# A fused Perceiver layer on one core: stage 1 in another order, an fp32r gate, and a scratch tensor by channel quarters

## The reference, cut to what matters

```python
def _L0_xattn_ref(encoder_hc, decoder_hq, w_sim, b_sim, W_qv, b_qv):      # hc = layernorm(x), hq = context
    w1, w2, w3 = (w_sim[:d], w_sim[d:2 * d], w_sim[2 * d:])
    Sim = (hc @ w1)[:, :, None] + (hq @ w2)[:, None, :] + einsum('bid,bjd->bij', hc * w3, hq) + b_sim[0]
    hq_hat = einsum('bij,bjd->bid', softmax(Sim, axis=2), hq)
    hc_bar = einsum('bi,bid->bd', softmax(max(Sim, axis=2), axis=1), hc)[:, None, :]
    return concatenate([hc, hq_hat, hc * hq_hat, hc * hc_bar], axis=-1) @ W_qv + b_qv

def _L0_attn_ref(x, A, Bp, Cp, Dp, Wg, bg, gamma, beta):                  # x = layernorm(x)
    xg = x * sigmoid(x @ Wg.T + bg)
    # for each channel: s = s @ A + xt * Bp;  y = s . Cp + Dp * xt, over 32 tokens
    return layernorm(y + xg) * gamma + beta

def _L0_ffn_ref(x, fast_b, w_fc, w_proj, u, v, gate):                     # x = layernorm(x)
    h = bitlinear(x, w_fc) + gate * (x @ v.T @ fast_b.T @ u.T)            # ternary weights times a row scale
    return bitlinear(relu(h) ** 2, w_proj)
```

## Time and profile before

| what | value |
|---|---|
| median of three runs | 539.21 us (538.7 to 541.0) |
| profiled execution | 538.89 us, span 536.4 us, clock 0.98 |
| instructions | 13420 |
| busy: PE, DVE, ACT, POOL | 479.4, 419.9, 359.4, 343.9 us |
| stage 1, step 1's hq transposes to step 32's | 28.9 to 334.3 us |
| first scan block | 339.7 us |

### The profile page before, as it was taken

How to read it: one execution, slowest core, us unless ns; L and a number is a source line. 1 busy time by engine, 2 the same in 40 slices (tenths; PEclk the granted TensorE clock), 3 DMA queues, 4 the chain that set the end, 5 groups by cost and what they waited for, 6 DMA issues and landing times. The chain is left out here.

```text
span 536.4 us, 13420 instructions
## 1 busy us (share of the span) xinstructions
PE 479.4 (89%) x4310; PEld 402.2 (75%) x4310; DVE 419.9 (78%) x1159; ACT 359.4 (67%) x854; POOL 343.9 (64%) x444
## 2 busy tenths in 40 slices
PE   2397799999999999999999996876799999999996
PEld 2275687888887877687787875765588888888885
DVE  1398888888888999999998884457677987988654
ACT  2555578676876767677676766555578768768753
POOL 1377767676775757756756664503578878888653
PEclk9789999999999999999999999998899999999999
DMA  6734445756584555555645568259502022011102
GB/s 206 197 114 149 138 151 160 219 156 217 145 234 136 177 169 139 191 146 139 199 136 144 194 200 178 60 133 218 125 1 79 1 80 79 26 55 39 41 1 78
DMA packets 81316, 70.38 MB, mean 131 GB/s; under 512 B 39760, under 2 KB 64608, under 8 KB 81248
## 3 DMA queue, kind: packets, MB, share of 16 engines
q1 hardware_dynamic: 81248, 69.54, 45.4%
HBM read 56.87 MB, written 12.65 MB: 130 GB/s over the span
## 5 line engine op out<-in xcount | busy, mean ns | idle before, releaser
L1647 POOL TENSOR_TENSOR sq_lo<-scan_x,sq_hi 128x512 fp32r<-128x512 f32 x63 | 82.7, 1313 | 33.6 <-ACT sq_hi L1619 33.6
L705 PE MATMUL turn_ps<-ident,ctxn 128*128 128x128 f32 x512 | 70.3, 282 | 4.4 <-DMA ctxn<-in_ctx 4.4
L933 ACT COPY ctxT<-turn_ps 128x512 f32<-128x512 f32 x128 | 68.2, 583 | 5.4 <-PE turn_ps L705 5.4
L705 PEld LDWEIGHTS turn_ps<-ident,ctxn 128*128 128x128 f32 x512 | 58.2, 144 | 18.0 <-issue 13.2
L1611 ACT ACTIVATE relu<-fc_ps,fc_square 128x512 f32<-128x512 f32 x64 | 43.8, 684 | 31.0 <-PE fc_ps L1545 30.9
L1689 DVE SCALAR_TENSOR_TENSOR scan_x<-fc_ps,relu 128x512 f32<-128x512 f32 x64 | 43.8, 684 | 26.0 <-ACT relu L1611 25.5
L1121 POOL TENSOR_TENSOR hc_lo<-hc_probT,hc_hi 128x256 fp32r<-128x256 f32 x32 | 23.4, 731 | 61.0 <-ACT hc_hi L942 60.9
L1541 PE MATMUL fc_ps<-xn_hi,fc_T 128*128 128x512 f32 x128 | 52.1, 407 | 2.1 <-DVE scan_x L1689 2.1
L1107 POOL TENSOR_TENSOR rstd<-ve,neg_half 128x1 f32<-128x1 f32 x64 | 35.2, 550 | 27.6 <-DVE ve L1331 17.7
L1541 PE MATMUL fc_ps<-xn_lo,fc_T 128*128 128x512 f32 x128 | 51.1, 399 | 0.0
L1113 POOL TENSOR_TENSOR proj_in<-proj_in,below 128x512 f32<-128x512 f32 x31 | 49.3, 1592 | 0.0
(11 more groups left out here) (227 smaller groups left out, 1400.8 us busy)
## 6 DMA issues: line engine op xcount, KB each, us to landing
ctxn<-in_ctx SPq DMA_DIRECT2D x32, 1024.0 KB, 5.5
resid<-in_x SPq DMA_DIRECT2D x32, 128.0 KB, 5.2
ctx_end<-in_ctx SPq DMA_DIRECT2D x32, 128.0 KB
gated_tokens<-gated SPq DMA_DIRECT2D x32, 128.0 KB, 6.2
scan_x<-gated_tokens SPq DMA_DIRECT2D x60, 64.0 KB, 4.9
out<-resid SPq DMA_DIRECT2D x7, 512.0 KB, 3.1
scan_tokens<-scan_x SPq DMA_DIRECT2D x12, 256.0 KB, 5.1
y_in<-scan_tokens SPq DMA_DIRECT2D x4, 512.0 KB, 4.8
```

The source lines that it names most:

```text
L705: mm = pe.transpose(turn_ps[b % 2][:, (c * JT + t) * P:(c * JT + t + 1) * P], ctxn[p][:, b, t, c * P:(c + 1) * P], ident[:, :])
L933: act.copy(ctxT[:, b, :, 0:J - 1], turn_ps[b % 2][:, :].rearrange("p (k j) -> p k j", k=KD)).then_inc(ctxT_copied, 1)
L1647: pool.tensor_tensor(sq_lo[:, m, :], sq[m % SQ], sq_hi[:, m, :].bitcast(F32), ALU.subtract).then_inc(sq_lo_done, 1)
```

## The change

What it does, part by part:

1. TensorE's step has another order: context 0 and 1, prob's transposes, pool, projection of hc, context 2 and 3, attend, score, z's transposes, hq's transposes, projection of hb, hc's transposes of the next group, gate, projections of hq and hcq. A projection waits for its lo half only in front of the matmuls that read it.
2. The gate is 6 fp32r matmuls with zT_hi, zT_lo, wgT_hi, wgT_lo. VectorE makes zT_lo every step.
3. The context has three buffers; the third is lent from rows 0 to 15 of `toeplitz`, which is zeroed in eight parts, six in steps 4 to 9 and two in step 31.
4. The first loads come in another order, and wqv_hi waits for W_qv alone and is made in step 1 (as is wqv_lo, after hcqT).
5. The ternary halves of w_fc alternate over steps 17 to 32 and stand ahead of hq on VectorE; magnitudes and scale come two steps earlier.
6. The state product stands at the end of GpSimd's step; steps 3, 4 and 5 have a second one ahead of hb_lo; the product with C comes in step 29.
7. On ScalarE hc's copy of the next group and hcwT stand before and behind the softmax exponential, and hc_hi at the end.
8. VectorE's step has another order, given in the diff.
9. In the end of stage 1 the placing, turn_z and the gate of the last group stand elsewhere between the scan blocks.
10. The y scratch is ordered by quarters of the channels: stores have 8 KB contiguous for each partition, a y load is four DMAs with pieces of 256 B; y load 0 is issued ahead of the last `gated` store.

```diff
+        def y_load(sp, c):
+            piece, part = divmod(c, 2)
+            for r in range(CH):
+                src = bass.AP(tensor=scan_dram.tensor, offset=piece * PB * L * D + (part * TOK + r * P) * CQ,
+                              ap=[[CQ, P], [PB * L * CQ, NB], [1, CQ]])
+                sp.dma_start(y_of(c)[:, r, :].rearrange("p (q d) -> p q d", q=NB), src).then_inc(y_loaded[c % 2], 16)
...
-            ctxn = [sb(f"ctxn{p}", [P, NB, JT, D], scope=s1) for p in range(2)]
+            ctxn = [sb(f"ctxn{p}", [P, NB, JT, D], scope=s1) for p in range(DEEP - 1)]
+            ctxn.append(toeplitz[:, 0:LENT, :].rearrange("p (b t k) j -> p b t (k j)", b=NB, t=JT))
...
-            FC_FIRST, LOW_GROUP, MAGS, SCALE_GROUP, TERNARY = 4, 15, 14, 18, 19
+            FC_FIRST, LOW_GROUP, LOW_IN, MAGS, SCALE_GROUP, TERNARY = 3, 15, 20, 12, 16, 17
...
+            def state_at_end(g):
+                return g - 1 + sum(t <= g for t in TWICE) if 1 <= g <= LAST_STATE else None     # TWICE (3, 4, 5), LAST_STATE 28
...
                 sp.wait_ge(scan_copied, BLOCKS)
-                store_piece(sp, 0, 0, PB // 2, first_stored[0])
-                store_piece(sp, 0, PB // 2, PB // 2, first_stored[1])
+                store_half(sp, 0)                    # 4 DMAs of 16 partitions x 8 KB
+                store_half(sp, 1)
+                sp.wait_ge(first_stored[0], 16 * NB)
+                y_load(sp, 0)
                 step(GROUPS + 1, 0, ())              # stores the last gated
-                sp.wait_ge(first_stored[0], 16 * NB)
-                sp.dma_start(y_in[:, :, :], scan_dram[0:TOK, :].rearrange("(r p) d -> p r d", p=P)).then_inc(y_loaded[0], 16)
-                sp.wait_ge(gated_stored[1], 16 * (GROUPS // 2))
-                scan_load(sp, GROUPS - 1, 1)
...
                 for i in range(1, PIECES - 1):
                     sp.wait_ge(scan_copied, (i + 1) * BLOCKS)
+                    if i == PIECES - 2:
+                        sp.wait_ge(gated_stored[1], 16 * (GROUPS // 2))
+                        scan_load(sp, GROUPS - 1, 1)
+                        sp.wait_ge(first_stored[1], 16 * NB)
+                        y_load(sp, 1)
+                    store_piece(sp, i)
...
+                def project_hc(g):
+                    at_least(pe, hc_hi_ready, g)
+                    at_least(pe, x1_ready, g - 1)
+                    project((hc_hi, hc_lo), 0, hc_lo_ready, g, first=True).then_inc(hc_projected, 1)
...
+                def sum_gate(g):
+                    pe.wait_ge(zT_hi_ready, g + 1)
+                    pe.wait_ge(zT_lo_ready, g + 1)
+                    for i, (part, w) in enumerate(((zT_hi, wgT_hi), (zT_hi, wgT_lo), (zT_lo, wgT_hi))):
...
+                    if g + 1 < GROUPS:              # ScalarE
+                        copy_hc(g + 1)
                     if has_a:
                         act.activation(prob[p][:, :], score_ps[:, 0:J], ACT.Exp, bias=neg_max[:, 0:1],
                                        accum_out=row_sum[:, 0:1]).then_inc(exp_done, 1)
+                    if g + 1 < GROUPS:
+                        weigh_hc(g + 1)
+                    if has_a:
                         act.activation(top_e[:, :], best[:, :], ACT.Exp, bias=neg_top[:, 0:1])
...
+                    if g in TWICE:                  # GpSimd
+                        state_product(state_at_end(g) - 1)
...
                         low_part(hcq_lo[:, :, :], hcqT[:, :, :], hcq_hi[:, :, :], hcq_hi_ready, hcq_lo_ready, g)
+                    if state_at_end(g) is not None:
+                        state_product(state_at_end(g))
+                    if ZERO_FIRST <= g < ZERO_FIRST + ZERO_PARTS - LENT_PARTS:      # 4 to 9
+                        zero(g - ZERO_FIRST + LENT_PARTS)
...
# VectorE's step, by the tiles that it writes:
- x1, bn2, mv2, ve2, bn1, mv1, ve1, nmr2, hbT, hq, hc, dots, hcqT, weights(g), state_sum, hq_lo, neg_max, best, bestT, neg_top, gate_in, row_rec, prob, top_rec, pick, gated
+ x1, bn2, mv2, ve2, bn1, mv1, ve1, state_sum, nmr2, hbT, hc, weights(g), hq, dots, neg_max, zT_lo, hcqT, hq_lo, best, bestT, neg_top, gate_in, row_rec, prob, top_rec, pick, gated
```

## The result

The new kernel takes 557.75 us (median of 4, 556.8 to 558.6), the old one 538.96 beside it: a ratio of 1.0346, interval 1.0324 to 1.0368. I had forecast 540 with a range of 524 to 549. The profiled execution has a span of 556.3 us, 19.9 more than before.

| stretch | before | after | difference | forecast |
|---|---|---|---|---|
| first hq transposes | 28.9 | 25.3 | -3.5 | -7.8 |
| 31 periods | 305.4 | 330.7 | +25.3 | +12.3 |
| last hq transposes to the scan | 5.4 | 3.2 | -2.3 | -2.0 |
| scan to the first FFN chunk | 31.5 | 32.3 | +0.8 | -1.8 |
| stage 3 | 165.2 | 164.7 | -0.5 | 0 |

What follows compares the result with a forecast made beforehand. The prediction took a loop through TensorE and VectorE, with prob held, to set the new period. Start -7.8, periods +12.3, way to the first chunk -2.0 -2.3 +0.5: +0.7 on 538.9, forecast 540 us, range 524 to 549.

Steps and rivals of the forecast that it cites:

- The period: Stage 1 groups: plain period 9.68 us against 9.10, bounds 8.8 to 9.9; the 31 periods together 317.7, 12.3 more.
- Through TensorE: Loop from hq_lo over prob, pick, x1, attend, score, zT and zT_lo back to hq_lo: 9.66 us in a plain group.
- prob held: VectorE's prob waits for the end of GpSimd's state product: 0.87 us a group.
- The gate: Six fp32r matmuls take TensorE 0.71 to 0.77 us, four fp32 ones 0.80; zT_lo adds 0.33 on VectorE.
- hcwT: ScalarE's weigh_hc (0.77) ahead of top_e: top_rec waits 0.66 us for top_eT even with prob free; loop 9.47 without the hold.
- The start: First hq transposes at 21.1 us instead of 28.9: -7.8, with 5.99 from TensorE's stop and 1.8 from wqv_lo.
- Between the stages: Last gated store leaves near when its tile is ready, as y loads offset faster stores: +0.5 us, bounds -3 to +3.
- The scan's own part: TensorE's stops for z and zT inside the scan go, as turn_z and the gate stand two blocks later: -2.3 us.
- A: Faster rival: GpSimd's instructions don't reach prob and hc, prob slips in ahead of the product: 524 us, 515 to 530; chance 0.27.
- B: Slower rival: ternary halves on VectorE still caught by GpSimd, 0.45 lost in 16 groups: 547 us; chance 0.20.
- C: Loads rival: context 1 lands late at the start, or 256 B y loads delay the scan load: 543 to 549 us; chance 0.08.

Runs made afterwards that it cites:

- e2: New kernel with ScalarE's hcwT of the next group made behind top_e and top_eT, state product still at the step's end: 549.33 us.
- e13: e5 with hcwT where the old kernel had it, behind prob's copies and ahead of those of context 2 and 3: 521.04 us.
- e15: e13 with the gate back in plain fp32: 510.74 us.
- e16: New kernel with only the gate back in plain fp32: 540.75 us.
- e5: New kernel with GpSimd's state product moved from its step's end to right behind hc_lo of the next step: 534.11 us.
- e6: e5 with hcwT behind top_eT as well: 538.58 us.
- e9: e5 with ScalarE's top_e, top_eT and tanh ahead of hcwT: 539.73 us.
- e4: New kernel with y load 0 issued behind the store of the last gated tile on the SyncE queue: 557.63 us.
- e11: Old kernel with only the state product at the end of GpSimd's step from step 4 on, its state sum in the next step: 536.26 us.

## Why the prediction was wrong

- **The period, the step that failed most.** "*Through TensorE.* From hq_lo's start: 1.51 to prob, 1.14 for it held, 0.19, 0.20 and 0.34 for top_rec, pick and gated". prob held was right (1.24, forecast 1.23), and the loop was the right one: with pick free e2 shows 9.68 in a plain group. But I took pick's 0.20 from the old kernel, where GpSimd is idle beside it, and never asked what GpSimd does at that time in the new order. hc_lo starts as pick does, and pick takes 0.84: +0.55 in 14 of the groups 10 to 27, 10.24 in a plain one. These 14 make 7.7 us, and the 18 groups took 183.3 for 175.4 forecast. The sum of all periods was missed by 13 (317.7 forecast, 330.7 measured): the other 5 are 3.3 in groups 6 to 9, where the sum has no term for TensorE's clock falling to half in groups 6 and 9 (the undisturbed 7 and 8 took 10.77, forecast 10.74), and 2 in the first five and last four.
- **The gate.** "TensorE's own sum goes from 9.10 to at best 8.7" priced the part by TensorE and added zT_lo as 0.33 to VectorE. It stands on the loop with its wait and costs a plain group 0.2 (9.02 in e13, 8.80 in e15) to 0.5 (9.76 with pick free, 9.2 to 9.5 in e16) for 0.07 saved; taking it out brings 10.3 us in e15, and 17 in e16, the pick holds that go with it included. The terms were all in my sum; what I didn't draw from them is that the part by itself is a loss.
- **hcwT.** "The hold is not all of it: weigh_hc (0.77) now stands between ... ", with 0.66 as the price and 9.47 without the hold, was right in kind: e5 has top_rec wait 0.42 and a period of 9.55. e6 and e9 show that it costs wherever something stands behind it on ScalarE.
- **The start.** "I take 1.8 us of it as having reached them" failed: first transposes at 25.3, not 21.1, nor at the 22.9 without that credit. The score now stands ahead of them, and TensorE works at half the rate here (eight context transposes at 17.17 in 1.92, later in 1.04). How long it does so differs between executions: e4's profile, with the same start, has the first transposes at 22.4, so up to 3 of the 4 us are not the order's. wqv_lo ends a wait behind them, as the 12.5 for group 1 had it (12.95 measured):

```profile
17.17 1.92 PE L733 MATMUL turn_ps<-ident,ctxn 128*128 128x128 f32 x8
...
28.70 0.50 PE L744 MATMUL qv_ps<-proj_T,hc_hi 128*128 128x256 f32 x2 [2.49 <-DVE fc_T L1453]
```

- **Between the stages.** "it leaves near when the tile is ready, as before: +0.5" failed: the last gated tile was ready at 370.4 and its store left at 374.7. The scan's own part was nearly right (10.75 to that tile, 12.4 before: -1.65 for -2.3). e4 shows that the queue's new order gives it back elsewhere; only the whole old order brings something, 0.7 and 2.1 us.
- **The rivals.** A (prob slips ahead) did not happen: prob's median is 1.24. B (halves caught) neither, but for one first and one second half of eight each: their medians are 0.346 and 0.480. The Trainium skill ("SBUF — State Buffer", Who interferes with whom) says that a VectorE instruction with two SBUF inputs can block too, against a GpSimd one that reads SBUF. In seven of the eight groups no GpSimd instruction was in flight when the second half started (252.30 in one, hb_lo at 252.74); in the eighth a copy was, and the half took 0.82, which agrees:

```profile
353.52 1.03 POOL L1191 COPY toeplitz<-ctxn 32x1024 f32<-32x1024 f32 x1
354.00 0.82 DVE L177 SCALAR_TENSOR_TENSOR fc_in<-fc_in,thresholds,xn 128x256 f32<-128x256 f32 x1
```

  C named the start and the scan load. Neither of its causes (context 1 late, slow y loads) is shown, but both places missed the forecast, by 7 us together.
- **The chances.** I gave "slower" 0.35 and ended the range at 549. The bound of the period that I wrote, 9.9, has no working, and leaves no room for a held pick: 9.68 + 0.55 is 10.23. A bound has to be taken with every short instruction of the loop held. That 9.68 was met within 0.1 where pick is free is in part luck: in the group shown the way from hq_lo to z's transposes, apart from pick, is 7.84 for 8.04, and zT with its handovers 0.61 for 0.40.

## What to carry to other kernels

When instructions are put in another order, lay GpSimd's timeline of the new order beside every VectorE instruction that it can hold, the four-column ones too: where a held one is on the loop the price is the rest of the GpSimd instruction, elsewhere it is far less (e11). Price a part by the engine that ends last after it, not by the one that it relieves. A late ScalarE instruction costs by what stands behind it in order, so put it where the engine idles and not ahead of a short one that others wait for: undoing two placements, the gate and two orders of loads and stores turned 3.5% slower into 5.8% faster.

## What the runs showed of the hardware

- An instruction of 4 columns is held like one of 257: pick 0.84 and prob 1.24. pick ends within 0.03 of hc_lo's end, prob 0.16 after the product's.
- Who is first is decided within 0.1 us. pick was held though its record starts 0.09 ahead of hc_lo's (135.59 and 135.68); in e16 it starts 0.10 ahead and takes 0.29. So it is in every profile here: the 37 held picks that start ahead of hc_lo do so by 0.04 to 0.10 and take 0.79 to 0.85, and the free ones start 0.10 to 0.38 ahead. The Trainium skill (the same page and section) says that whoever issues first gets the ports; the start in a record isn't that moment.

```profile
137.16 0.29 DVE L1485 TENSOR_SCALAR pick<-own_batch,top_e,top_rec 128x4 f32<-128x4 f32 x1
```

```profile
137.26 0.78 POOL L1170 TENSOR_TENSOR hc_lo<-hc_probT,hc_hi 128x256 fp32r<-128x256 f32 x1 [0.36 <-ACT hc_hi L1088]
```

- Four fp32 matmuls of 128x256 and six fp32r ones cost TensorE nearly the same here, 1.10 and 1.03 us with the pair behind them.
